# Product-key top-k searches of the last stage cut into fourteen pieces, two per unit, one of them between weighting and summing the gathered rows

## What is computed

```python
sim = einsum('pbnhd,pkhd->pbnhk', q, pk_keys)      # 2 halves x 8 heads x 64 keys
scores, idx = top_k(sim, 16)                       # in each of the 16 groups
index = idx[0][..., :, None] + (idx[1] * 64)[..., None, :]
score = scores[0][..., :, None] + scores[1][..., None, :]
final_scores, pk_idx = top_k(score, 16)            # of the sums of a head
final_scores = softmax(final_scores)
k = einsum('bnhk,bnhkd->bnhd', final_scores, keys_table[ind])
v = einsum('bnhk,bnhkd->bnhd', final_scores, values_table[ind])
```

## Time and profile before

| what | value |
|---|---|
| time, median of 3 runs | 8379.15 us |
| lowest and highest run | 8332.54 and 8438.06 us |
| profiled execution, first to last instruction | 8270.5 us |
| POOL busy | 4767.7 us (58%) |
| DVE busy | 4630.4 us (56%) |
| PE busy | 2929.9 us (35%) |
| ACT busy | 1276.4 us (15%) |
| moved by the gathers (queue q0) | 272.90 MB, 13.2% of the DMA engines |
| granted clock in the last stage | 0.5 of full speed |

### The profile page before, as it was taken

One profiled execution on the slowest core, in us unless ns is written; L12 is line 12 of the kernel. 1 busy time (PEld: TensorE's weight loads), 2 busy tenths in 40 slices (PEclk: granted clock), 3 DMA queues, 4 the chain that ended last, 5 costly groups with the idle time before them and its releaser, 6 DMA issues.

```text
span 8270.5 us, 48114 instructions
## 1 busy us (share of the span) xinstructions
PE 2929.9 (35%) x9994; PEld 1847.9 (22%) x9994; DVE 4630.4 (56%) x12390; ACT 1276.4 (15%) x2443; POOL 4767.7 (58%) x4418
## 2 busy tenths in 40 slices
PE   3569989511112223222322232322223322221127
PEld 1247654200001112111211121211112212111125
DVE  4667754555555555665565555654656566544542
ACT  1246643200000001000100010100001101000002
POOL 4135520077777666666676666765666677657761
PEclk7579876555555555555555555555555555555555
DMA  1000002121121112111211121111111211111110
GB/s 24 10 5 4 5 26 78 57 60 44 44 60 45 40 43 59 41 43 40 58 44 41 40 57 42 45 41 54 41 41 43 59 45 44 41 36 48 44 40 10
DMA packets 202975, 339.37 MB, mean 41 GB/s; under 512 B 117359, under 2 KB 117940, under 8 KB 202688
## 3 DMA queue, kind: packets, MB, share of 16 engines
q0 software_dynamic: 135168, 272.90, 13.2%
q1 hardware_dynamic: 67520, 63.39, 2.4%
HBM read 305.60 MB, written 30.43 MB: 41 GB/s over the span
## 4 chain that ended last, share of the span: by engine, by line
DVE 33%; issue 25%; another core or an unknown queue 10%; POOL 8%; PE 3%; DMA 1%; ACT 1%; DVEq 0%; SPq 0%; ACTq 0%; POOLq 0%
POOL sq_rows L1726 8%; DVE sq_kv L2059 8%; DVE sq_rows L2057 5%; DVE sq_is_cand L2014 2%; DVE sq_row_f L2016 2%; DVE sq_is_cand L2012 2%; DVE sq_top_at L1980 2%; DVE sq_sim_rest L1979 2%; DVE sq_d_negmax L1927 1%; DVE sq_top L1976 1%; DVE sq_top_at L1988 1%; DVE sq_diag_out L1926 1%; PE sq_ps_d L1754 1%; DVE sq_c_inv L2073 1%
## 5 line engine op out<-in xcount | busy, mean ns | idle before, releaser
L1726 POOL DMA_INDIRECT sq_rows<-in_L_ffn_table,sq_row x4096 | 4290.0, 1047 | 2285.5 <-issue 1308.9
L1765 PE MATMUL sq_ps_c<-sq_kT,sq_qT 64*128 64x128 f32 (+2 forms) x384 | 225.3, 688 | 2243.8 <-ACT sq_prob L1869 1775.3
L2059 DVE TENSOR_REDUCE sq_kv<-sq_rows 128x128 f32<-128x2048 f32 x256 | 921.3, 3599 | 19.9 <-DVE sq_rows L2057 10.0
L1754 PE MATMUL sq_ps_d<-sq_d_q,sq_d_k 64*128 64x512 f32 x512 | 506.1, 1131 | 983.8 <-ACT sq_exp_out L1863 615.9
L1765 PEld LDWEIGHTS sq_ps_c<-sq_kT,sq_qT 64*128 64x128 f32 x384 | 104.8, 315 | 2451.4 <-ACT sq_prob L1869 1862.3
L2057 DVE TENSOR_TENSOR sq_rows<-sq_rows,sq_weight 128x2048 f32<-128x2048 f32 x256 | 585.5, 2287 | 113.5 <-DMA sq_rows<-in_L_ffn_table,sq_row 89.2
L1869 ACT ACTIVATE sq_prob<-sq_ps_c,sq_c_negmax 128x128 f32<-128x128 f32 (+3 forms) x256 | 135.0, 527 | 3285.2 <-DVE sq_c_negmax L2068 2800.4
L952 POOL TENSOR_TENSOR at_psum_p<-at_prob 128x1024 f32<-128x1024 f32 x128 | 302.0, 2360 | 316.1 <-ACT at_prob L903 312.6
L1863 ACT ACTIVATE sq_exp_out<-sq_ps_d,sq_d_bias 128x512 f32<-128x512 f32 x256 | 175.9, 687 | 1911.4 <-DVE sq_d_bias L1930 1320.1
L1754 PEld LDWEIGHTS sq_ps_d<-sq_d_q,sq_d_k 64*128 64x128 f32 x512 | 126.8, 310 | 1150.3 <-ACT sq_exp_out L1863 695.2
L1783 PE MATMUL sq_ps_o<-sq_kv,sq_probT 128*128 128x64 f32 x1280 | 304.4, 404 | 117.8 <-issue 63.1
(11 more groups left out here) (345 smaller groups left out, 6254.9 us busy)
## 6 DMA issues: line engine op xcount, KB each, us to landing
sq_rows<-in_L_ffn_table,sq_row POOLq DMA_INDIRECT x4096
qkvT<-exp_rows SPq DMA_DIRECT2D x32, 768.0 KB, 3.3
sq_d_q<-qkvT SPq DMA_DIRECT2D x8, 1024.0 KB
sq_d_k<-qkvT SPq DMA_DIRECT2D x8, 1024.0 KB
sq_d_v<-qkvT SPq DMA_DIRECT2D x8, 1024.0 KB
tok_rows<-in_L_tok_hash_rows,tok_idx_now POOLq DMA_INDIRECT x128
tok_chars<-in_x SPq DMA_DIRECT2D x8, 128.0 KB
h<-tok_h_tok SPq DMA_DIRECT2D x8, 128.0 KB, 2.0
```

What stands on the lines that cost most here:

```text
L1726: pool.indirect_dma_start(rows[j % GSLOTS][:, k, :], None, w2["table"], bass.IndirectOffsetOnAxis(row[t % 2][:, h, k:k + 1], 0)).then_inc( ...
L1754: pe.matmul(ps_d[u % 2][:, :], d_k[f, h // 2, t * P:(t + 1) * P], d_q[f, h // 2, :], start=True, stop=True).then_inc(S["d_scores"], 1)
L1765: pe.matmul(ps_c[u % 2][:, 0:t * P], q, kT[f, h // 2, 0:t * P], start=True, stop=True)
L2059: s.did(dve.tensor_reduce(kv[r.par][:, t, :, h, :], slot[:, :, :].rearrange("p j (m c) -> p m c j", m=2), AX.X, ALU.add))
```

## The change

`best8` and `next8` take a range of groups instead of a count. The waits at their ends move to the start of `next8` and `candidates` and to the users behind. `choose` has 14 pieces: `best8` over groups 0-3, 4-7, 8-11, 12-15 (pieces 0 to 3; the last raises `sim_used`), `next8` over 8 groups each (4, 5), `candidates` (6), `best8` over 4 heads each (7, 8), `next8` over the 8 heads with the centring of the weights (9), and `table_rows` over two heads each (10 to 13; the last makes the row numbers, raises `row_ready` and normalises the weights). Unit h takes piece 2h where the single piece stood. `mix` is cut into `weigh` (the wait and L2057's product) and `add_rows` (L2059's sum and the release of the buffer), and piece 2h + 1 stands between the two.

```diff
                 def best8(groups, values, at, source, rest):
-                    for g in range(groups):
+                    for g in groups:
                         s.did(dve.max(values[:, g, 0:8], source[:, g, :]))
                     s.wait()
-                    for g in range(groups):
+                    for g in groups:
                         s.did(dve.match_replace(rest[:, g, :], values[:, g, 0:8], source[:, g, :], LOW))
                         s.did(dve.max_index(at[:, g, 0:8], values[:, g, 0:8], source[:, g, :]))
-                    s.wait()
...
                     if piece == 0:
                         held(dve, S["sim_ready"], r.at(TT, t + 2 + r.early), dve_passed)
-                        best8(GROUPS, top, top_at, sim[b], sim_rest)
-                        dve.sem_inc(S["sim_used"], 1)
-                    elif piece == 1:
-                        next8(GROUPS, top, top_at, sim_rest)
-                    elif piece == 2:
+                    if piece < 4:
+                        best8(range(4 * piece, 4 * piece + 4), top, top_at, sim[b], sim_rest)
+                        if piece == 3:
+                            s.wait()
+                            dve.sem_inc(S["sim_used"], 1)
+                    elif piece in (4, 5):
+                        next8(range(8 * (piece - 4), 8 * (piece - 3)), top, top_at, sim_rest)
+                    elif piece == 6:
                         candidates()
-                    elif piece == 3:
-                        best8(HEADS2, best, best_at, cand, cand_rest)
-                    elif piece == 4:
-                        next8(HEADS2, best, best_at, cand_rest)
+                    elif piece in (7, 8):
+                        best8(range(4 * (piece - 7), 4 * (piece - 6)), best, best_at, cand, cand_rest)
+                    elif piece == 9:
+                        next8(range(HEADS2), best, best_at, cand_rest)
...
-                    elif piece == 5:
-                        table_rows(range(HEADS2 // 2))
-                    elif piece == 6:
-                        table_rows(range(HEADS2 // 2, HEADS2))
...
+                    elif piece in (10, 11, 12, 13):
+                        s.wait()
+                        table_rows(range(2 * (piece - 10), 2 * (piece - 9)))
+                        if piece == 13:
+                            s.wait()
...
-                def mix(r, u):
+                def weigh(r, u):
...
                     s.did(dve.tensor_tensor(slot[:, :, :], slot[:, :, :], bc(weight[t % 2][:, h, :], 2, KV), ALU.mult))
+
+                def add_rows(r, u):
+
+                    t, h = divmod(u, HEADS2)
+                    slot = rows[u % GSLOTS]
                     s.wait()
                     s.did(dve.tensor_reduce(kv[r.par][:, t, :, h, :], slot[:, :, :].rearrange("p j (m c) -> p m c j", m=2), AX.X, ALU.add))
...
-                        if j < UN and r.chosen(t):
-                            choose(r, t, h)
+                        if j < UN and r.chosen(t) and 2 * h < 14:
+                            choose(r, t, 2 * h)
                         if r.cau and j < UN:
                             causal_max(r, j)
                         if r.cau and j >= 2:
                             causal_normalise(r, j - 2)
                         if r.mix and j < UN:
-                            mix(r, j)
+                            weigh(r, j)
+                        if j < UN and r.chosen(t) and 2 * h + 1 < 14:
+                            choose(r, t, 2 * h + 1)
+                        if r.mix and j < UN:
+                            add_rows(r, j)
```

More of the change, by code:

```diff
@@ L1973, in best8, with next8, candidates @@
                 def best8(groups, values, at, source, rest):
-                    for g in range(groups):
+                    for g in groups:
                         s.did(dve.max(values[:, g, 0:8], source[:, g, :]))
                     s.wait()
-                    for g in range(groups):
+                    for g in groups:
                         s.did(dve.match_replace(rest[:, g, :], values[:, g, 0:8], source[:, g, :], LOW))
                         s.did(dve.max_index(at[:, g, 0:8], values[:, g, 0:8], source[:, g, :]))
+                def next8(groups, values, at, rest):
                     s.wait()
-                def next8(groups, values, at, rest):
-                    for g in range(groups):
+                    for g in groups:
                         s.did(dve.max(values[:, g, 8:16], rest[:, g, :]))
                     s.wait()
-                    for g in range(groups):
+                    for g in groups:
                         s.did(dve.max_index(at[:, g, 8:16], values[:, g, 8:16], rest[:, g, :]))
+                def candidates():
                     s.wait()
-                def candidates():
                     s.did(dve.tensor_copy(top_at_f[:, :, :], top_at[:, :, :]))
@@ L2052, in mix @@
-                def mix(r, u):
+                        table_rows(range(2 * (piece - 10), 2 * (piece - 9)))
+                        if piece == 13:
+                            s.wait()
+                            s.did(dve.tensor_copy(row[b][:, :, :], row_f[:, :, :]))
+                            s.wait()
+                            dve.sem_inc(S["row_ready"], 1)
+                            dve.wait_ge(S["weight_exp"], r.at(TT, t + 2 + r.early))
+                            s.did(dve.tensor_reduce(wsum[:, :], weight[b][:, :, :], AX.X, ALU.add))
+                            s.wait()
+                            s.did(dve.reciprocal(wsum[:, :], wsum[:, :]))
+                            s.wait()
+                            s.did(dve.tensor_tensor(weight[b][:, :, :], weight[b][:, :, :], bc(wsum[:, :], 2, TOPK), ALU.mult))
+                            s.wait()
```

10 lines of the change are left out of this document (removed).

## The result

The changed kernel is slower, not faster: 8464.6 us (median of 4 runs, 8438.4 to 8500.0) against 8355.9 us of the kernel before in the same comparison, a ratio of 1.019 [1.010, 1.028] (the brackets are a 95% interval, here and below). The sign is clear of the interval, a loss of 2% isn't. Ratios are made from fast executions alone; where slower ones of the kernel before were left out, a ratio isn't the quotient of the two medians given. The prediction said 7760 us and a range of 7540 to 8240 us. The profiled execution has a span of 8498.1 us, 228 us more than that of before.

A forecast was written before the change was run, and what follows sets the result against it. POOL's gathers bound the kernel, its stops for DVE being winnable. Gathers of 5120 + 538 + 175 = 5833 us replace 6449, 616 less; span 7654 us plus 109 gives 7760 us, range 7540 to 8240 us.

The forecast's parts named there:

- the crawl: DVE's searches: idle time before each short instruction while POOL gathers; a search of 8.5 us then takes 71.3 us.
- (b): One piece between product and sum: the product breaks POOL's run, so most crawl goes; 20 us a tile stays.
- (a): Smaller search pieces on DVE: same instructions, work about 117 us a tile; a free piece of 20 takes 2.1 us.
- (c): Later buffer release in `add_rows`: free while a buffer is free, else up to 6 us in two units a tile.
- (d): `row_ready` raised behind unit 6's product: 10 us of cover, so no cost unless exceeded, then the excess once a tile.
- (e): A round's start: POOL stops 25 us for DVE at each of seven such places, 175 us.
- first-search "issue" time: Idle time before the first search's match and index instructions on DVE: to fall from about 40 us a tile to under 20.
- the waits for L2061's release: POOL's waits for a buffer freed by DVE: to fall from 577 to under 200 us, the longest staying at rounds' starts.
- Rival 3: POOL's stops end the crawl; without them all four DVE searches crawl: 950 us slower, 9330 us; chance 0.07.
- Rival 1: Stalls belong to the instructions: some 57 us a tile remain over units 0 and 1; 8010 us; chance 0.18.
- Rival 2: Gain taken up elsewhere: DVE waits for PE and ACT, or late `row_ready` loses 620 us; 8380 us; chance 0.11.

The follow-up runs named there:

- one_gather: The kernel before with one gather per unit instead of sixteen, the other fifteen rows left out: 5687.8 us, 0.663 of the kernel before.
- pool_break: The kernel before with a 128x1024 MEMSET on POOL and a wait for it ahead of each unit's gathers: 8034.3 us, 0.967; again 8073.3 us, 0.975.
- both_first: The changed kernel with both pieces of a unit at its start, none between product and sum: 8862.7 us, 1.032 of the kernel before; again 8780.3 us, 1.062.
- break_changed: The changed kernel with a 128x1024 MEMSET on POOL and a wait for it ahead of each unit's gathers: 8002.7 us, 0.933 of the kernel before.

## Why the prediction was wrong

**What bounds the kernel** was read rightly as far as it went: POOL at 1.25 us a gather, its stops for DVE, and DVE slowed by the crawl rather than busy. The observation that the crawl needs POOL gathering without a break was right too; `one_gather` and `pool_break` show it, and so does the table of crawl against POOL's runs.

**The step that failed is (b): "I take the crawl to go for most pieces."** It rested on "DVE sending many short instructions meanwhile" as a second condition, with an onset 13.5 us after a product, and on "Each product holds POOL for about 1.9 us (2.89 - 0.95), which is a break." Neither held. The price that the sum gave it, 20 us a tile, came out as 62.2 us, where the kernel before has 57.9:
- There is no onset that counts from a product or from a burst. It counts from POOL's last stop, some 20 us in; the search read for the 13.5 us had POOL gathering since 4139 us. The timeline above has hand-overs of 1.95 and 3.97 us directly behind a product, and within pieces of 20 instructions the steps begin at the eighth to tenth behind the MAX8. `one_gather` has the long burst and no crawl.
- The product isn't break enough. Its neighbour gather at 4388 us took 2.38 us in the changed kernel, and the crawl went on, though a MEMSET of 0.97 us with a wait behind it lifts much of it (1052 steps of 1 to 2.2 us became 430). What tells these two apart I can't say: the one stretches a gather, the other stands between two.
- So whole pieces still crawl; only the form changed, from short steps to hand-overs.

**What I had not seen at all is the hand-over.** The earlier trace rows showed the crawl on a search, whose instructions follow one another without waiting, and I took 1.3 us per instruction for its price. Units with waits between instructions pay 5 to 6.5 us at each long one on average, and up to 11. The kernel before had one long search under the crawl, in which POOL ran out of free buffers and the crawl ended; the change spreads it. Mean time from the product of unit h to the next one, tiles 4 to 27:

| kernel | h=0 | 1 | 2 | 3 | 4 | 5 | 6 | 7 to next tile | tile |
|---|---|---|---|---|---|---|---|---|---|
| before | 13.5 | 12.4 | 17.5 | 20.6 | 23.1 | 21.4 | 8.7 | 87.3 | 204.5 |
| changed | 37.8 | 44.2 | 20.0 | 15.1 | 22.3 | 20.1 | 15.8 | 38.1 | 213.4 |
| `both_first` | 48.3 | 16.5 | 22.9 | 33.6 | 20.7 | 21.6 | 8.4 | 56.7 | 228.7 |
| `break_changed` | 22.9 | 24.4 | 23.4 | 20.5 | 22.4 | 24.5 | 22.6 | 35.4 | 196.1 |

The 87 us place went down by 49, as meant, and units 0 and 1, which took 13 and 12 us, went up by 24 and 32.

The other steps:
- **(a)** held: instructions and DVE's busy time are the same (464.4 us a round against 467.1), and a free piece takes about 2.4 us where 2.1 was worked out.
- **(c)** held in sum: waits for buffers 572.6 us against 577.4, though in 49 stops in place of 31; the later release isn't where the time went.
- **(d)** `row_ready` grew to 562 us after the first, in 25 waits of 22 us, where the sum had nothing. It wasn't the order behind the product: with the same order `break_changed` has 44 us. DVE as a whole reached unit 6 late, by the crawl in units 7, 0 and 1.
- **(e)** and the sum: 175 us for POOL's stops came out as 1135 by POOL's waits. The other terms, tried where their premise holds, were sized well: in `break_changed` the gathers took 4453.2 - 4096 x 0.947 = 574 us beyond their plain time (538 forecast), and 5120 + 574 + 371 for the breaks + 100 of stops = 6165 us against a stretch of 6190 (1646.5 to 7836). The 109 us that the forecast added between span and time aren't a fixed part: in every execution on record the time is 1.7 to 2.2 us above its own span, and the profiled execution of the kernel before was simply a shorter one than those that were timed. That shifts the forecast by at most 109 us and isn't why it failed.
- **Sign by sign:** first-search "issue" time fell as named, to a third (some 13 us a tile), and the loss moved; the waits for L2061's release (now L2070) stayed; `row_ready` waits grew, which the prediction itself had named as what would make it wrong; POOL's busy time fell instead of rising by 100; DVE's waits for the gathers' DMAs rose from 89 to 140 us, not over 1000; a tile takes 211 us.
- **Rivals.** Rival 3 named half of the mechanism, "POOL's stops are what ends the crawl", and the side. Its condition, that POOL never stops, didn't come: POOL stopped more often and for longer. So its size (9330) was wrong, with all four searches crawling throughout; of the 950 us that it gave, some 216 came, and by hand-overs, which it didn't have. Its counter-argument, "a product breaks POOL's run in every unit", is the error of step (b) again. Rival 1 had the losses moving to units 0 and 1, which they did, but at an unchanged price per instruction and so with a gain. Rival 2 named late row numbers, and they came late, though less of it (562 us) than its 620 and not by their place behind the product, as (d) shows.

One gather per unit shows a straight run of 80 instructions without idle time, so straight code runs unhindered here when POOL is quiet, and doesn't while POOL gathers. The rule of the Trainium skill that the prediction weighed ("Runtime: NRT & Kernel Launch", section "Instruction fetch mechanics": fetching runs ahead of a straight run and is hidden) agrees with the measurement only for the first of these.

Fetching isn't what the crawl waits for, as far as the trace tells: its records of the two instruction queues (q8 and q14) have one packet at 4247.4 us (8192 bytes, 0.5 us) and the next at 4333.8 us, none within the crawl of 4249.9 to 4317.4.

**What stays open:** which resource POOL's indirect DMAs share with the other engines' instructions and semaphore steps, and whether it is the number of DMAs or of their rows; why the kernel before takes 8332 to 8368 us on chip 13 and 8580 on chips 8 and 14 while the versions with the larger break came out at 8002 to 8073; and whether another queue for the gathers would be free of it, which wasn't tried. One rival no run here touches: every time on record has the span of a traced execution beside it, so the recording itself, whose semaphore steps come late or are missing in the crawl, may take part in it.

## What to carry to other kernels

Here the idle time marked "issue" between short independent instructions was a state, not a price of these instructions: where you see it, find what other engine is doing in it, and ask what each waiting instruction will pay when work is moved into that state. Cutting a long run into pieces adds waits, and waits were the dearest thing here (5 to 6.5 us on average, up to 11); test first whether the state itself can be ended, as by one MEMSET per unit that cost POOL 1.45 us and gave 2.5 to 3.3% on the kernel before and, across batches, over 5% on the changed one. If a neighbour's stop is what ends the state, letting it run less far ahead can be faster than letting it run on.

## What the runs showed of the hardware that I had not expected

- While POOL issued an indirect DMA every 1.25 us, from some 20 us after its last stop to 8 to 12 us after its next, DVE's short instructions came in steps of 0.7 and 1.4 us, and a wait on a semaphore that DVE itself had raised took up to 11.06 us. SP's queue is slow in the same stretches; its timeline in the kernel before, with POOL gathering:

```profile
4084.99 0.69 SPq L1693 DMA_DIRECT2D sq_d_q<-qkvT  x1
4089.19 0.69 SPq L1693 DMA_DIRECT2D sq_d_k<-qkvT  x1
4093.39 1.39 SPq L1693 DMA_DIRECT2D sq_d_v<-qkvT  x1
4097.58 0.70 SPq L1694 DMA_DIRECT2D sq_d_x<-h  x1
```

They are issued 4.2 us apart, six times the 0.7 us of DVE's steps.

- Halving the bytes of each gather changed nothing (1.000). A MEMSET of 128x1024 with a wait, every 16 gathers, lifted much of it (0.967 and 0.975 in two batches, crawl per tile 34.1 us in place of 57.9); one of 128x64 gave 0.959 on another chip with 58.7 us of crawl left.
- The bounds are far apart for the same program on DVE: a tile takes 125 us with one gather per unit and 204.5 us with sixteen, of which POOL's own gathering asks 160 us.
